# Eight batch rows through four layers on one core: gathers moved beside other phases, keys and values multiplied head by head, projections without copies

## What is computed

```
xn = layernorm(x)
x  = x + attention_l(xn) * silu(experts_l(xn))
```

## Time and profile before

| | us |
|---|---|
| median of 3 runs | 3543.29 |
| the 3 runs | 3523.14, 3543.29, 3543.45 |
| the profiled execution, its own time | 3538.98 |
| span of the profiled execution | 3537.2 |
| outside the span | 1.8 |

### The profile page before, as it was taken

How to read it: one execution, slowest core, us unless ns; L and a number is a source line. 1 busy time by engine, 2 the same in 40 slices (tenths; PEclk the granted TensorE clock), 3 DMA queues, 4 the chain that set the end, 5 groups by cost and what they waited for, 6 DMA issues and landing times. The chain is left out here.

```text
span 3537.2 us, 56353 instructions
## 1 busy us (share of the span) xinstructions
PE 2484.3 (70%) x19990; PEld 1783.3 (50%) x19990; DVE 2055.8 (58%) x4732; ACT 1366.1 (39%) x2376; POOL 794.3 (22%) x745
## 2 busy tenths in 40 slices
PE   6999964634675679041599999979234577968994
PEld 3656643421674568021355555549222456966763
DVE  6667664358377124737788888854264894451115
ACT  4444422224011013121388888854115323423332
POOL 0000002200473112723240000002527851105100
PEclk9999986856555579575699999999658798977997
DMA  5000002200074026200100000007201005721000
GB/s 181 1 1 1 1 0 71 42 1 26 0 207 81 3 86 207 64 12 1 36 33 1 1 2 1 1 22 228 77 19 39 9 0 149 223 81 47 25 0 29
DMA packets 156996, 177.64 MB, mean 50 GB/s; under 512 B 55621, under 2 KB 126026, under 8 KB 155882
## 3 DMA queue, kind: packets, MB, share of 16 engines
q1 hardware_dynamic: 135866, 131.59, 13.1%
q0 software_dynamic: 20912, 43.22, 4.0%
HBM read 126.70 MB, written 48.04 MB: 49 GB/s over the span
## 5 line engine op out<-in xcount | busy, mean ns | idle before, releaser
L2442 DVE CUSTOM_DVE_ANT_0 decayed_sd<-decayed_sc,decayed_decay 128x512 f32<-128x512 f32 x512 | 331.7, 686 | 86.0 <-PE decayed_sc L2319 85.8
L2397 ACT ACTIVATE decayed_pr<-decayed_sd,decayed_shift 128x512 f32<-128x512 f32 x512 | 339.0, 713 | 49.2 <-DVE decayed_shift L2449 49.0
L2331 PEld LDWEIGHTS decayed_tr<-all_ident,decayed_pr 128*128 128x128 f32 x2048 | 223.5, 140 | 175.3 <-ACT decayed_pr L2397 101.1
L2331 PE MATMUL decayed_tr<-all_ident,decayed_pr 128*128 128x128 f32 x2048 | 276.8, 278 | 11.1 <-ACT decayed_pt L2404 10.8
L460 PE MATMUL experts_up<-experts_xt,experts_w 128*128 128x256 f32 x1140 | 272.3, 386 | 0.0
L460 PEld LDWEIGHTS experts_up<-experts_xt,experts_w 128*128 128x128 f32 x1140 | 211.6, 194 | 24.8
L386 POOL DMA_INDIRECT rows_in<-L_T,all_slot x128 | 149.2, 1166 | 137.9 <-SPq L2246 82.2
L2456 DVE COPY decayed_pt<-decayed_tr 128x512 f32<-128x512 f32 x256 | 173.3, 685 | 2.6 <-PE decayed_tr L2331 2.6
L437 POOL DMA_DIRECT2D rows_out<-experts_y x121 | 87.4, 722 | 384.9 <-DVE experts_y L522 218.4
L694 PEld LDWEIGHTS moe_down<-moe_w,moe_h 128*128 128x128 f32 x1024 | 131.6, 192 | 56.2 <-issue 55.2
L762 DVE SCALAR_TENSOR_TENSOR all_S<-moe_down,L3b_soft_gate,all_S 128x128 f32 x128 | 42.8, 351 | 191.6 <-PE moe_down L694 191.0
(11 more groups left out here) (512 smaller groups left out, 5554.9 us busy)
## 6 DMA issues: line engine op xcount, KB each, us to landing
experts_w<-in_L_experts SPq DMA_DIRECT2D x78, 384.0 KB, 3.4
experts_w<-in_L_experts SPq DMA_DIRECT2D x43, 579.0 KB, 4.0
experts_tok<-rows_in SPq DMA_DIRECT2D x121, 128.0 KB, 3.4
rows_out<-experts_y POOLq DMA_DIRECT2D x121, 128.0 KB, 3.4
L_b<-bands SPq DMA_DIRECT2D x24, 384.0 KB, 4.8
rows_in<-linear_zero SPq DMA_DIRECT2D x43, 128.0 KB, 1.9
experts_w<-in_L_experts SPq DMA_DIRECT2D x8, 514.0 KB, 3.6
solveb_band<-bands SPq DMA_DIRECT2D x8, 384.0 KB, 4.7
```

The lines of the kernel that those rows point to most:

```text
L2331: last = pe.transpose(tr[u % TURNED][:, t * P:(t + 1) * P], pr[:, u % RING, t * P:(t + 1) * P], m.ident[:, :])
L2397: act.activation(pr[:, u % RING, :], sd[:, u % RING, :], ACT.Exp, bias=shift[:, u % RING:u % RING + 1]).then_inc(exp_ready, 1)
L2442: dve.tensor_tensor_reduce(out=sd[:, u % RING, :], in0=sc[h][:, :], in1=decay[:, qt, :], scale=1.0, scalar=-3.0e38, op0=ALU.mult, op1=ALU. ...
```

## The change

Four edits. (1) In the linear phase the key-value section multiplies head by head: V is stored by head with its own column of ones (65 columns), each product of a pair becomes two, on 64 columns of K each, and the second head's result lands on PSUM partitions 64 to 127; ACT's copies keep their sizes. (2) Of layer 1's 64 gathers, those of blocks 0 to 4 (40) stay in `stats`, those of blocks 5 to 7 (24) are issued by POOL in `gatemlp`. (3) Layer 2's experts run ahead of `out2`; POOL issues the gathers of blocks 0 and 1 (16) in `out2`, and the other 48 in `mix2`. (4) `project_phase` is written out without loops: no POOL copies, PE reads the source in place, transposes run one block ahead of the multiplications, and the first one ahead of the wait for the weight.

```diff
-def gather_rows(pool, m, rows, collected):
-    for n in range(NB):
+def gather_rows(pool, m, rows, collected, first=0, end=NB):
+    for n in range(first, end):
         for t in range(n * TPB, (n + 1) * TPB):
             for k in range(2):
                 pool.indirect_dma_start(rows[k][:, t, :], None, m.rows_out, bass.IndirectOffsetOnAxis(m.SLOT[:, k, t:t + 1], 0)).then_inc(collected[n], 16)
...
-    VW = P + 1
+    VW = DH + 1
...
-        V = s.sb("V", [P, TPB, PAIRS, VW])
+        V = s.sb("V", [P, TPB, 2 * PAIRS, VW])
...
                         for t in range(TPB):
-                            last = pe.matmul(nd[g % 2][:, 0, k * VW:(k + 1) * VW], K[:, t, p * P:(p + 1) * P], V[:, t, p, :],
-                                             start=(t == 0), stop=(t == TPB - 1))
+                            for h in range(2):
+                                last = pe.matmul(nd[g % 2][h * DH:(h + 1) * DH, 0, k * VW:(k + 1) * VW], K[:, t, p * P + h * DH:p * P + (h + 1) * DH],
+                                                 V[:, t, 2 * p + h, :], start=(t == 0), stop=(t == TPB - 1))
...
-                        act.activation(KV[part, 2 * g:2 * g + 2, part], src[:, :, part], ACT.Copy)
-                        last = act.activation(KV[part, 2 * g:2 * g + 2, P + k:P + k + 1], src[:, :, P:VW], ACT.Copy)
+                        act.activation(KV[part, 2 * g:2 * g + 2, part], src[:, :, 0:DH], ACT.Copy)
+                        last = act.activation(KV[part, 2 * g:2 * g + 2, P + k:P + k + 1], src[:, :, DH:VW], ACT.Copy)
...
         @block.gpsimd
         def _(pool):
-            pool.sem_inc(stage_ready, 1)
-            with pool.Fori(0, NB // 2) as i:
...
+            if pool_beside is not None:
+                pool_beside(pool)
 
         @block.tensor
         def _(pe):
-            pe.wait_ge(loaded, 16 * loads)
...
+            def transpose(n):
+                if n >= 2:
+                    pe.wait_ge(stage_ready, n - 1)
+                for t in range(TPB):
+                    last = pe.transpose(turned[n % 2][:, t * P:(t + 1) * P], src[:, n * TPB + t, :], m.ident[:, :])
+                last.then_inc(turned_ready, 1)
+
+            def multiply(n):
+                if turn:
+                    pe.wait_ge(stage_ready, n + 1)
+                if n >= 2:
+                    pe.wait_ge(out_done, n - 1)
+                for t in range(TPB):
+                    rows = stage[:, n % 2, t * P:(t + 1) * P] if turn else src[:, (n * TPB + t) * P:(n * TPB + t + 1) * P]
+                    last = pe.matmul(ps[n % 2][:, t * P:(t + 1) * P], rows, w[:, :], start=True, stop=True)
+                last.then_inc(ps_ready, 1)
+
             if turn:
...
+                transpose(0)
+            pe.wait_ge(loaded, 16 if bias is None else 32)
+            for n in range(NB):
+                if turn and n + 1 < NB:
+                    transpose(n + 1)
+                multiply(n)
...
-            branch_stats_phase(nc, "stats", m, branches, b[5], b[0], b[1], lambda pool: gather_rows(pool, m, rows1, collected1), m.spill)
-            gate_mlp_phase(nc, "gatemlp", m, d, b[1], b[0], b[5])
+            branch_stats_phase(nc, "stats", m, branches, b[5], b[0], b[1], lambda pool: gather_rows(pool, m, rows1, collected1, 0, 5), m.spill)
+            gate_mlp_phase(nc, "gatemlp", m, d, b[1], b[0], b[5], lambda pool: gather_rows(pool, m, rows1, collected1, 5, NB))
...
-            project_phase(nc, "out2", m, m.S, d["L2_wo"], m.S, turn=True, bias=d["L2_bo"])
             routed_phase(nc, "experts2", m, 8, 2, "glu", d["L2_experts"], act_fn=ACT.Silu, sent=sent2)
...
-            collect_mix_phase(nc, "mix2", m, rows2, [a.sem(f"collected{n}") for n in range(NB)], gather=True)
+            collected2 = [a.sem(f"collected{n}") for n in range(NB)]
+            project_phase(nc, "out2", m, m.S, d["L2_wo"], m.S, turn=True, bias=d["L2_bo"],
+                          pool_beside=lambda pool: gather_rows(pool, m, rows2, collected2, 0, 2))
+            collect_mix_phase(nc, "mix2", m, rows2, collected2, gather=lambda pool: gather_rows(pool, m, rows2, collected2, 2, NB))
```

More of the change, by code:

```diff
@@ L823, in gather_rows, with collect_mix_phase @@
                 pool.indirect_dma_start(rows[k][:, t, :], None, m.rows_out, bass.IndirectOffsetOnAxis(m.SLOT[:, k, t:t + 1], 0)).then_inc(collected[n], 16)
-def collect_mix_phase(nc, phase, m, rows, collected, shared=None, gather=False):
+def collect_mix_phase(nc, phase, m, rows, collected, shared=None, gather=None):
     with Scope(nc, phase) as s:
@@ L835, in _ @@
         def _(pool):
-            if gather:
-                gather_rows(pool, m, rows, collected)
+            if gather is not None:
+                gather(pool)
         @block.scalar
@@ L1998, in _, with gate_mlp_phase @@
             link(dve.transpose(stats_t[:, :], stats[:, :]))
-def gate_mlp_phase(nc, phase, m, d, stats_t, logits_t, logits):
+def gate_mlp_phase(nc, phase, m, d, stats_t, logits_t, logits, gather):
     with Scope(nc, phase) as s:
@@ L2019, in _ @@
             sp.dma_start(b[:, :], d["L1_gate_b"]).then_inc(loaded, 16)
+        @block.gpsimd
+        def _(pool):
+            gather(pool)
         @block.tensor
@@ L2141, in _, with project_phase @@
             link(dve.transpose(out_t[:, :], a[:, :]))
-def project_phase(nc, phase, m, src, weights, out, turn=False, bias=None, gate=None):
+def project_phase(nc, phase, m, src, weights, out, turn=False, bias=None, gate=None, pool_beside=None):
     with Scope(nc, phase) as s:
@@ L2155, in project_phase @@
         ps = s.banks("ps", 2)
-        loaded, raw_ready, turned_ready, stage_ready, ps_ready, out_done, gated = map(
-            s.sem, ("loaded", "raw_ready", "turned_ready", "stage_ready", "ps_ready", "out_done", "gated"))
+        loaded, turned_ready, stage_ready, ps_ready, out_done, gated = map(
+            s.sem, ("loaded", "turned_ready", "stage_ready", "ps_ready", "out_done", "gated"))
         block = s.enter_context(nc.Block())
-        loads = 2 if bias is not None else 1
         three = lambda t: t.rearrange("p (t n) -> p t n", n=P)
-        src_block = (lambda n: src[:, bass.ds(n * TPB, TPB), :]) if turn else (lambda n: three(src[:, bass.ts(n, 512)]))
         @block.sync
@@ L2183, in _ @@
         @block.tensor
         def _(pe):
-            pe.wait_ge(loaded, 16 * loads)
-            if turn:
[L2187 to L2205, removed]
+            def transpose(n):
[4 more added lines that the diff above has]
+                last.then_inc(turned_ready, 1)
@@ L2209, in _ @@
             def _(act):
[L2210 to L2216, removed]
+                for n in range(NB):
+                    act.wait_ge(turned_ready, n + 1)
+                    if n >= 2:
+                        act.wait_ge(ps_ready, n - 1)
+                    act.activation(stage[:, n % 2, :], turned[n % 2][:, :], ACT.Copy).then_inc(stage_ready, 1)
```

42 lines of the change are left out of this document (15 added, 27 removed).

## The result

The changed kernel takes 3460.4 us in the median of four runs (3456.39 to 3467.64), against 3543.37 for the kernel before: a ratio of 0.9776 (95% interval 0.9754 to 0.9798). Forecast were 3468.0 us with a range of 3448 to 3500. Timed a second time, beside the last experiment, it took 3472.42 in the median of five runs (ratio 0.9793, 0.9765 to 0.982). The profiled execution is the slowest of the first four, 3467.64 us (span 3465.8), so profile stands against profile with 3467.64 - 3538.98 = -71.3; the sum of the steps was -71.0.

What follows compares the result with a forecast made beforehand. No engine bounds it everywhere: phases end at barriers, each set by its own engine or hand-overs. Terms -23.7 - 21.3 - 1.9 - 18.3 - 5.8 = -71.0 from 3538.98 gave 3468.0 us, range 3448 to 3500.

Steps and rivals of the forecast that it cites:

- Linear phase, -23.7: Key-value section by head: paired products run side by side, saving 2.9 us in seven rows and 3.4 in the last.
- Rival A: Linear phase: the two heads' products follow each other, section stays 7.3 us, whole kernel 3491.7 us; chance 0.14.
- rival B: Linear phase: each of 128 instructions pays load and pass, section grows to 15.0 us, kernel 3552.7 us; chance 0.03.
- Stats, -21.3: Layer 1's stats with 40 gathers: DVE instead of POOL ends the phase, next begins at 1498.5 instead of 1519.83.
- Rival D: Gatemlp: the 24 moved gathers do not hide, 72 us more than the phase, kernel 3540 us; chance 0.03.
- Layer 2's tail, -18.3: Layer 2's out2 and mix2: out2 2.0 us longer with 16 gathers, mix2 20.3 us shorter without them.
- 5.5 for the end: Out2: time from POOL's last gather to the next phase, 5.5 us, within out2's forecast 26.0 us.
- rival C: Out2: the 5.5 us after the last gather are not paid, out2 about 20 us, whole 3462.5; no separate chance.
- the pace of mix2: Mix2: each gather taken as 1.268 us, so 16 gathers fewer save 20.3 us.
- out1, -1.9: Projection out1 without POOL's copies: 0.8 us saved at the start and 0.15 for each of 7 hand-overs.
- out3, -5.8: Projection out3: first transposes precede the weight, blocks then take about 1.45 us, end at 2941.6 against 2947.44.
- 3, 5.7 and a low run's 15.8: Range's lower end, 3448: 3 us more in out1 and out3, 5.7 in out2, and a low run.

Runs made afterwards that it cites:

- the last experiment: Changed kernel with layer 2's attention cut in two halves, the decay table loaded in the second half, the residual stream awaited in mix2: 3448.42 us, ratio 0.9741.

## Why the prediction was right, step by step

**What bounds the kernel** was read rightly: the phases' ends. Every stage that the windows pointed to gave within 2.4 us what was expected of it. Together they gave 73.7 us where 71.0 were forecast, and the phases that were left at 0 gave 2.4 back, so that the sum is off by 0.3; part of this closeness is luck.

*Linear phase, -23.7, came as -24.85.* The two heads of a pair do run side by side: 4.07 us for the section, 3.65 being taken for the 64 pairs and the rest lying at the section's start, middle and end. L1359 started 4.85 us after the section (5.0 forecast), DVE's search took over as the last wait, as said. A row's period fell by 3.06 where 2.9 was forecast, which makes nearly all of the 1.15 that it came out better. Rival A is refuted by the row of the changed trace and rival B too, and the orders of the products show why it held: what runs beside is set by the order of issue, alternate or in runs of up to four. The rule of the Trainium skill that was weighed there ("TensorE: Matmul & The Clock Gate", Part 3, The mechanism), that weight loads overlap running products only for another group of rows, does not agree with this trace: in its records weight loads and products of the two heads, on the same 128 rows, start 6 or 7 ns apart. The Trainium skill's "TensorEngine Tiling (Array Packing)", Key Properties, says that different tiles can load and multiply in parallel, and the trace agrees.

*Stats, -21.3, came as -20.98.* POOL was through 18 us before the barrier; gatemlp's cover held, 55.14 with 24 gathers against 55.19 without. Rival D is refuted: not one gather in gatemlp took over 0.97 us. POOL's end after 40 gathers was 3.33 and not the 5.5 taken, which changes nothing, since DVE ends the phase. Three of the four held gathers of stats remain (POOL's last gather starts ahead of the fourth L1992); one of them, and DVE before and beside it:

```profile
1435.16 4.42 DVE L1990 TENSOR_REDUCE stats_mean<-L_T 128x128 f32<-128x4096 f32 x1
...
1439.92 4.42 DVE L1992 TENSOR_TENSOR L_b<-L_T,L_b 128x4096 f32<-128x4096 f32 x1
1440.37 4.81 POOL L823 DMA_INDIRECT L_rows<-rows_out,all_slot  x1 [0.30 <-issue]
```

The gather lasts 4.81 us beside L1992, which has two inputs in SBUF and lasts 4.42; beside L1990, as long and with one input, the gathers take their 0.95. That agrees with the Trainium skill's "SBUF — State Buffer", SBUF: two separate sides, where a DVE instruction with two SBUF inputs and a GpSimd operation that reads SBUF take a shared port in turns, each for its whole instruction.

*Layer 2's tail, -18.3, came as -19.2*, from two terms that failed in opposite directions. "5.5 for the end" of out2 was taken from the 64 gathers of stats; after 16 it was 2.3. That is rival C in part, but not by its reason (work beside): to the barrier the phases with 16, 32 and 64 gathers show 2.28, 3.02 and 5.33, and POOL's DRAIN shows the same with work beside, so the number is what counts. And the pace of mix2 was taken as 1.268 for each gather and came as (2519.83 - 2458.87)/47 = 1.297, 1.4 us over 48: 19 of the 48 gathers stand beside DVE's work and take 1.05 us in the mean (up to 1.46), the others 0.95; before, it was 20 of 64, at 1.00. The forecast's pace was also the fastest of five: with 64 gathers mix2 shows 1.268 to 1.317.

*out1, -1.9, came as -2.7; out3, -5.8, as -5.9.* Out1 varies by 1.2 us over the three profiles with the loop (15.76, 14.53, 15.20) and by 1.8 over the nine without; the means differ by 2.0, so the term was right within what can be read. Out3 has the forecast pace: the first transposes run before the weight, then DVE's two instructions set 1.4 us a block.

*The median.* It stands 7.6 us under the forecast, inside the range, while the profile agrees to 0.3. The twelve profiles, all with the same scan, show it at 144.3 to 170.5 us, and a second timing gave 3472.42, 4.4 above the forecast. What made the lower runs of the first timing lower is not shown, since only the profiled runs can be looked into: they lie 6.5 to 11.3 us under the profiled one, while the profiles show the scan at 144 to 147 or at 165 to 171 and layer 3's causal attention at 141 or at 149 to 150. Two figures of the range do not come out of their own terms: 3, 5.7 and a low run's 15.8 under the forecast make 3443.5, not 3448, and half of the linear gain is 11.9, not 14. The forecast doesn't hang on either.

## What to carry to other kernels

Where phases end at barriers, look for the engine that ends each one and for a neighbour in which that engine has nothing to do; a queue such as POOL's gathers moved there for nothing here (24 gathers in gatemlp), and the neighbour's own window told beforehand that they fit. Small products on separate halves of the array ran side by side here even with all rows shared, as long as the issue order alternated between the halves at least every four instructions (two float32 products); at eight the section was 1.0 us longer, at sixteen 2.4. And before a step is called small or large by a median, see which phase varies between executions of the same code: here one phase did by 26 us, more than any single edit gained.

## What the runs showed that was not expected

The delta scan's length: 144.3, 146.6, 164.7, 164.7, 165.1, 167.5, 167.8, 167.9, 168.1, 168.2, 168.4 and 170.5 us in the twelve profiles, with mean granted clocks of 0.64 for the first and 0.58 for the last, and the same instructions. Layer 3's causal attention shows the like on a smaller scale, 141.3 and 141.5 us in two profiles and 148.9 to 149.9 in the others. What tips a run to one side was not tried.

POOL's end after gathers grows with their number, from 2.23 us after 16 to 5.29 after 64, whatever runs beside. And PE's overlap of the two halves in runs of 8 and 16 stops at exactly three instructions, whatever the length of the run.
